# Two cross-attention layers on one core: inner matmuls padded to 128 rows and columns, softmax probabilities split two key tiles at a time

## The reference, cut to what matters

```python
# layer 0: 8 heads of 64 channels; x and context are (16, 128, 512)
q = einsum('oc,bcn->bon', Wq, x);  kv = einsum('oc,bcm->bom', Wkv, context)
sim = einsum('bhdi,bhdj->bhij', q, k)          # 512 queries x 512 keys
attn = softmax(sim, axis=-1)
out = einsum('bhij,bhdj->bhid', attn, v);  y = einsum('oc,bcn->bon', Wout, out) + bout
# layer 1: 8 heads of 16 channels, biases, rotary embedding on q and k, scale 1/sqrt(16)
```

## Time and profile before

| | |
|---|---|
| time, median of 3 runs | 3264.57 us (3253.11 to 3277.23) |
| span of the profiled execution | 3264.8 us |
| layer 0 attention | about 80 to 1065 us |
| layer 1 attention | about 1725 to 2520 us |
| busy over the whole span | TensorE 2477.9, VectorE 2300.3, ScalarE 1842.6, GpSimd 1806.1 us |
| mean granted TensorE clock | 0.881 of full speed |

### The profile page before, as it was taken

One profiled execution on the slowest core, in us unless ns is written; L12 is line 12 of the kernel. 1 busy time (PEld: TensorE's weight loads), 2 busy tenths in 40 slices (PEclk: granted clock), 3 DMA queues, 4 the chain that ended last, 5 costly groups with the idle time before them and its releaser, 6 DMA issues. The chain is left out here.

```text
span 3264.8 us, 41636 instructions
## 1 busy us (share of the span) xinstructions
PE 2477.9 (76%) x11034; PEld 962.1 (29%) x11062; DVE 2300.3 (70%) x3282; ACT 1842.6 (56%) x3160; POOL 1806.1 (55%) x1577
## 2 busy tenths in 40 slices
PE   2999999999999046676647888989888312999930
PEld 0333333333333023233221222222222311555510
DVE  4778878878877775675636999888996571666644
ACT  1888888888888012232225888888887301444410
POOL 1667767767767010110125889888887275333445
PEclk9999999999999568898876999899998556999975
DMA  4232222222220300000001111111110103777745
GB/s 111 54 61 57 48 60 58 49 60 59 49 57 18 154 14 1 0 0 0 0 24 36 36 31 31 35 31 31 35 29 7 55 1 105 245 244 241 242 143 171
DMA packets 145405, 219.01 MB, mean 67 GB/s; under 512 B 20232, under 2 KB 108808, under 8 KB 144144
## 3 DMA queue, kind: packets, MB, share of 16 engines
q1 hardware_dynamic: 130448, 175.83, 20.5%
q0 software_dynamic: 14848, 41.99, 4.7%
HBM read 125.41 MB, written 42.02 MB: 51 GB/s over the span
## 5 line engine op out<-in xcount | busy, mean ns | idle before, releaser
L354 POOL TENSOR_TENSOR a_p_l<-a_probs,a_p_h 128x512 f16<-128x512 f32 x1024 | 1190.5, 1175 | 416.7 <-ACT a_p_h L564 414.7
L631 DVE TENSOR_REDUCE a_negmax<-a_ps_max 128x1 f32<-128x512 f32 x1024 | 675.7, 682 | 106.7 <-PE a_ps_max L431 101.9
L558 ACT ACTIVATE a_probs<-a_ps_st 128x512 f32<-128x512 f32 x1024 | 593.6, 593 | 236.4 <-PE a_ps_st L43 228.5
L564 ACT ACTIVATE a_p_h<-a_probs 128x512 f16<-128x512 f32 x1024 | 635.2, 626 | 1.3
L465 PE MATMUL a_ps_o<-a_p_h,a_v_h 128*128 128x512 f16 x1024 | 402.9, 393 | 1.9 <-POOL a_p_l L354 1.9
L679 DVE RECIPROCAL a_sums<-a_sums 128x128 f32<-128x128 f32 x384 | 356.3, 938 | 20.1 <-ACT a_plain L576 20.1
L890 POOL TENSOR_TENSOR f_hl<-f_h,f_hh 128x2048 f16<-128x2048 f32 x16 | 65.1, 4071 | 375.5 <-ACT f_hh L994 375.5
L431 PE MATMUL a_ps_max<-a_k_st,a_q_st 48*128 48x512 f16 x512 | 210.9, 413 | 32.9 <-DVE a_negmax L631 16.6
L43 PE MATMUL a_ps_st<-a_q_st,a_k_st 68*128 68x512 f16 x512 | 208.7, 408 | 6.9 <-ACT a_probs L558 6.2
L467 PE MATMUL a_ps_o<-a_p_h,a_v_l 128*64 128x512 f16 x512 | 206.3, 403 | 0.0
L470 PE MATMUL a_ps_o<-a_p_l,a_v_l 128*128 128x512 f16 x512 | 205.8, 402 | 0.0
(11 more groups left out here) (293 smaller groups left out, 4717.7 us busy)
## 6 DMA issues: line engine op xcount, KB each, us to landing
s_raw<-in_guT SPq DMA_DIRECT2D x32, 768.0 KB, 5.7
m_y<-s_y SPq DMA_DIRECT2D x32, 768.0 KB, 4.8
a_k_hh<-a_qk_h SPq DMA_DIRECT2D x64, 256.0 KB, 5.1
a_ctx_in<-in_ctx SPq DMA_DIRECT2D x32, 256.0 KB, 2.6
a_q_hl<-a_qk_h SPq DMA_DIRECT2D x32, 256.0 KB, 4.4
a_q_hm<-a_qk_h SPq DMA_DIRECT2D x32, 256.0 KB, 4.7
a_q_hl<-a_qk_l SPq DMA_DIRECT2D x32, 256.0 KB, 5.0
a_k_lo<-a_qk_l SPq DMA_DIRECT2D x32, 256.0 KB, 5.0
```

The costliest lines, as they stand in the source:

```text
L354: pool.tensor_tensor(p_l[:, h % 2, j, :], probs[:, h % RAWS, j, :], p_h[:, h % 2, j, :], ALU.subtract).then_inc(p_split, 1)
L558: act.activation(probs[:, h % RAWS, j, :], ps_st[:, j % 2, :], ACT.Exp, scale=1.0 if L0 else DH1 ** -0.5).then_inc(exped, 1)
L564: act.activation(p_h[:, h % 2, j, :], probs[:, h % RAWS, j, :], ACT.Copy).then_inc(p_high, 1)
L631: dve.tensor_reduce(negmax[:, h % 2, t:t + 1], ps_max[:, t % 2, :], AX.X, ALU.max, negate=True).then_inc(maxed, 1)
```

## The change

Four things:

- Layer 0: `v_l`, 64 columns for each head before, has 128, of which 64 are filled with zeros once (a second memset on GpSimd, a second count of `cleared`), and its product with `p_h` writes all 128 rows of `a_ps_o`. VectorE writes the 64 columns inside the wider rows.
- Layer 1: the rows with the maxima move from partition 64 to 96 (`MR`), and `max_product` reads `MR` = 96 rows instead of 48, of which 48 to 95 are zeros. `score_products` reads 100 rows instead of 68.
- Both layers: `low_probs` and `high_probs` run over two key tiles at once (128 x 1024), and their counters `p_high` and `p_split` count pairs.
- ScalarE's order: the copy of tiles 0 and 1 stands behind the third exponential of the head, that of tiles 2 and 3 at the head's end, where four copies stood behind exponentials 1, 2, 3 and at the end. `normalise` stands behind the first pair on GpSimd, where it stood behind the first tile.

```diff
...
     NQK = 8 if L0 else 4
-    MR = 64
+    MR = 64 if L0 else 96
     STACKS = 12 if L0 else 6
...
         v_h = sb("v_h", [P, 2, KD, H, P], F16)
-        v_l = sb("v_l", [P, 2, KD, H, DH0 if L0 else P], F16)
+        v_l = sb("v_l", [P, 2, KD, H, P], F16)
         if not L0:
...
         SETS = 1 if L0 else 16
-        CLEARS = 1 if L0 else 4
+        CLEARS = 2 if L0 else 4
         block = ctx.enter_context(nc.Block())
...
-            def low_probs(batch, h, j):
-                need(pool, p_high, KD * (H * batch[0] + h) + j + 1)
-                pool.tensor_tensor(p_l[:, h % 2, j, :], probs[:, h % RAWS, j, :], p_h[:, h % 2, j, :], ALU.subtract).then_inc(p_split, 1)
+            def low_probs(batch, h, i):
+                need(pool, p_high, 2 * (H * batch[0] + h) + i + 1)
+                two = slice(2 * i, 2 * i + 2)
+                pool.tensor_tensor(p_l[:, h % 2, two, :], probs[:, h % RAWS, two, :], p_h[:, h % 2, two, :], ALU.subtract).then_inc(p_split, 1)
...
                 for h in range(H):
-                    for j in range(KD):
-                        low_probs(batch, h, j)
+                    for i in range(KD // 2):
+                        low_probs(batch, h, i)
                         m, p = normalised(batch, h)
-                        if j == 0 and m is not None and exists(m):
+                        if i == 0 and m is not None and exists(m):
                             normalise(m[0], p)
...
                 pool.memset(v_h[:, :, :, :, :], 1.0).then_inc(cleared, 1)
+                pool.memset(v_l[:, :, :, :, :].rearrange("p a k h n -> p a (k h) n").bitcast(F32), 0.0).then_inc(cleared, 1)
             else:
...
                 else:
-                    a, bb = q_st[0:3 * DH, par, h, c], k_st[0:3 * DH, par, h, :]
+                    a, bb = q_st[0:MR, par, h, c], k_st[0:MR, par, h, :]
                 nc.tensor.matmul(ps_max[:, t % 2, :], a, bb, start=True, stop=True).then_inc(max_scores, 1)
...
                         need(pe, v_out, n + 1)
-                need(pe, p_split, KD * g + j + 1)
+                need(pe, p_split, 2 * g + j // 2 + 1)
                 first, last_head = (L0 or h % 2 == 0) and j == 0, (L0 or h % 2 == 1) and j == KD - 1
...
                 if L0:
-                    nc.tensor.matmul(ps_o[0:DH0, u % 2, :], v_l[:, par, j, h, :], ph, start=False, stop=False)
+                    nc.tensor.matmul(o, v_l[:, par, j, h, :], ph, start=False, stop=False)
                     ins = nc.tensor.matmul(o, vh, pl, start=False, stop=last_head)
...
-                need(act, p_split, KD * (g - RAWS) + j + 1)
+                need(act, p_split, 2 * (g - RAWS) + j // 2 + 1)
                 need(act, scores, 4 * g + j + 1)
...
-            def high_probs(batch, h, j):
+            def high_probs(batch, h, i):
                 g = H * batch[0] + h
-                need(act, weighted, KD * (g - 2) + j + 1)
-                need(act, exped, 4 * g + j + 1)
-                act.activation(p_h[:, h % 2, j, :], probs[:, h % RAWS, j, :], ACT.Copy).then_inc(p_high, 1)
+                two = slice(2 * i, 2 * i + 2)
+                need(act, weighted, KD * (g - 2) + 2 * i + 2)
+                need(act, exped, 4 * g + 2 * i + 2)
+                act.activation(p_h[:, h % 2, two, :], probs[:, h % RAWS, two, :], ACT.Copy).then_inc(p_high, 1)
...
                         exponential(batch, h, j)
-                        if j > 0:
-                            high_probs(batch, h, j - 1)
+                        if j == 2:
+                            high_probs(batch, h, 0)
                         if j == 3:
...
                                 value_highs(nxt[0], nxt[1])
-                    high_probs(batch, h, KD - 1)
+                    high_probs(batch, h, 1)
                     if h == SPLIT and exists(n2):
...
                         vals = lambda a: a.rearrange("p (h d) -> p h d", h=H)
-                        dve.scalar_tensor_tensor(v_l[:, par, t - 8, :, :], vals(ps_misc[:, :]), 1 / WS, v_h[:, par, t - 8, :, 0:DH0],
+                        dve.scalar_tensor_tensor(v_l[:, par, t - 8, :, 0:DH0], vals(ps_misc[:, :]), 1 / WS, v_h[:, par, t - 8, :, 0:DH0],
                                                  ALU.mult, ALU.subtract).then_inc(lows, 1)
```

## The result

The changed kernel takes 3499.89 us (median of 4 runs, 3498.97 to 3504.75) against 3263.12 us (4 runs, 3253.11 to 3277.23): ratio 1.072, 95% interval 1.069 to 1.075. It is 7.2% slower; 3468 us was forecast, with a range of 3310 to 3590. The profiled span is 3497.3 us, 232.5 more than before's 3264.8.

The account below looks back on a forecast made before the run. Layer 0 was taken as bound by TensorE, layer 1 by nearly every engine in turn. Chain 117, layer 0 clock 32, layer 1 net 3, waits 30 and layer 1 clock 21 sum to +203 us: 3468 us, range 3310 to 3590.

Parts of the forecast that it names:

- layer 0 was forecast at +149: Layer 0's attention: 117 us from later pair results plus 32 us from TensorE's clock falling.
- layer 1 at +54: Layer 1's attention: 3 us net, 30 us of VectorE waits for GpSimd and 21 us of clock falls.
- The chain in layer 0: Layer 0: take-outs, projection and next exponentials wait behind pair copy, subtraction and normalisation; +7.8 us a batch, +117 us.
- the signs: Listed trace marks of being right: starts 0.22 us apart, layer 0 TensorE under 85% busy, heads_out waits, heads' lengths.
- Layer 0's clock: TensorE standing longer in layer 0 drops its clock, between 0 and 1 fall a batch; 32 us, range 0 to 64.
- The waits: Waits for heads_out: take-out 2.5 to 3.5 us, three times a batch; projection 3 to 5 (layer 0), 2 to 3 (layer 1).
- the forecast's 0.2 + 2: Layer 1, a batch: net +0.2 us from later projection against shorter TensorE slots, +2 us of VectorE waits for GpSimd.
- The clock's 21 us: Layer 1: clock falls rise from 4 to 9 in 15 batches, 4.3 us each; 21 us, at most 47.
- The 30 us of waits for GpSimd: Layer 1: four VectorE instructions a batch wait for longer GpSimd instructions; 2 us a batch, 30 us in all.
- Rival 1: Pair results arrive in time, so the padding's gain shows in both layers: 3163 us; chance 0.11.
- Rival 2: ScalarE's idle time absorbs half the layer 0 delay, only heads 3 and 7 lose: 3250 to 3300 us; chance 0.10.
- Rival 3: TensorE at 1.2 GHz for most of layer 0, heads 4 and 5 doubling from 6.6 to 13: 3570 us; chance 0.10.

Follow-up runs that it names:

- the run that keeps TensorE busy: Changed kernel plus unused products in layer 0 where TensorE stands, 14 in head 7 and 16 ahead of the output projection: 3448.2 us.
- padding alone: Kernel before with only the wider v_l and the 96 maxima rows, copies and subtractions one key tile at a time: 3249.9 us.
- the run with a gap: Kernel before with the padding only, plus a GpSimd wait in layer 1's head 0, ahead of the fourth subtraction, for VectorE's rotation addition: 3177.4 us.

## Why the prediction was right

Direction, place and mechanism hold. The sum (+203) is 30 us under the span's difference, but that it comes so near is partly luck: layer 0 was forecast at +149 and cost 203, layer 1 at +54 and cost 23, and the two misses cancel for the greater part. The stretch between the layers, 7 us longer, is in no term.

**The chain in layer 0, head by head.** The third exponential of each head after the change, ScalarE in order of time (the first is head 6's at 503.36, shown above):

```profile
513.13 0.60 ACT L560 ACTIVATE a_probs<-a_ps_st 128x512 f32<-128x512 f32 x1 [0.65 <-PE a_ps_st L43]
521.63 0.59 ACT L560 ACTIVATE a_probs<-a_ps_st 128x512 f32<-128x512 f32 x1
531.56 0.60 ACT L560 ACTIVATE a_probs<-a_ps_st 128x512 f32<-128x512 f32 x1 [0.88 <-POOL a_p_l L355]
538.68 0.60 ACT L560 ACTIVATE a_probs<-a_ps_st 128x512 f32<-128x512 f32 x1 [0.85 <-POOL a_p_l L355]
548.61 0.60 ACT L560 ACTIVATE a_probs<-a_ps_st 128x512 f32<-128x512 f32 x1 [0.87 <-POOL a_p_l L355]
563.77 0.59 ACT L560 ACTIVATE a_probs<-a_ps_st 128x512 f32<-128x512 f32 x1
570.75 0.60 ACT L560 ACTIVATE a_probs<-a_ps_st 128x512 f32<-128x512 f32 x1 [0.28 <-POOL a_p_l L355]
578.48 0.59 ACT L560 ACTIVATE a_probs<-a_ps_st 128x512 f32<-128x512 f32 x1
```

| step | predicted us | measured us |
|---|---|---|
| head 6 to 7 | 9.4 | 9.77 |
| 7 to 0 | 6.45 | 8.50 |
| 0 to 1 | 10.0 | 9.93 |
| 1 to 2 | 6.9 | 7.12 |
| 2 to 3 | 10.0 | 9.93 |
| 3 to 4 (with the projection) | 8.45 + 4.4 | 15.16 |
| 4 to 5, 5 to 6 | 6.8, 6.65 | 6.98, 7.73 |
| sum | 69.1 | 75.1 |

Of the 6.0 us of difference the two steps 7 to 0 and 3 to 4 have 4.4, and they are the two with a half-clock stretch: the projection is 2.66 us longer (6.09 against 3.43), and in head 7 twelve products start 0.43 apart instead of 0.22, 2.5 us, of which 2.05 show. So without the clock a batch would take some 70.4 us: **the chain is worth +9.1 a batch, not +7.8**. This is a working, not a measurement, but the run that keeps TensorE busy bears it out: there the step 7 to 0 takes 6.65 us and 6 to 7 takes 9.45, next to the prediction's 6.45 and 9.4. The chain's largest miss is head 5 to 6, 1.1 us. Heads 4 and 5 do take 6.60 us each on TensorE, but head 6's third exponential comes 5.56 us behind its transpose (at 572.92), where 4.4 was taken: ScalarE's pair copy of head 5 stands ahead of head 6's exponentials until 575.5, and an evacuation that waits for TensorE stands ahead of the third one:

```profile
577.98 0.60 ACT L531 ACTIVATE a_v_h<-a_ps_misc 128x512 f16<-128x512 f32 x1 [0.92 <-PE a_ps_misc L43]
```

Of the signs, TensorE's busy share in layer 0 is 81%, under the 85 named, and from transpose to transpose heads 2 and 3 are longer and 4 and 5 shorter, as said; head 0 isn't longer (6.92 us for 7.50), its delay shows in head 1 (8.94).

**Layer 0's clock** was mis-sized: 2.1 us a batch taken, about 4.7 by the working above, 70 us in all in place of 32. The prediction allowed for one fall a batch at most, and two came, so its range for the term (0 to 64) ended short. The run that keeps TensorE busy gives back 3.6 of the 4.7; the 0.9 us that its added products hold up the projection are most of the rest. Chain 137 and clock 70, less 3 in the first batch, make 204 us; 202.6 were measured.

**The waits** came as forecast: take-out 3.1 us, measured 2.97, three times a batch; projection about 4, measured 4.02; layer 1's projection 2 to 3, measured 3.06 to 3.3, a little more, against 0.80 before.

**Layer 1**: 54 us forecast, 23.3 measured. A batch without a fall went from 47.6 to 49.5, near the forecast's 0.2 + 2: head 4 with the projection is 1.5 us longer, heads 1 and 2 together 1.6, the others 1.3 shorter. The clock's 21 us aren't there, and this is the term that was too large: the mean granted clock of layer 1 is 0.94 against 0.93. Falls come in about every second batch, but those of before were as costly in all (98 us at half clock against 116). The layer's first batch, 8 us shorter than before, is in no term. The 30 us of waits for GpSimd can't be seen in VectorE's sum (668.45 us busy against 666.52); they moved. The rotation's addition, in head 1, went from a median of 694 ns to 1159, and L670 (now L673), which is hidden behind the projection, from 1161 to 422. That the longer additions make heads 1 and 2 longer is likely, but no run separates it:

```profile
L660 DVE TENSOR_TENSOR a_rot_a<-a_rot_a,a_rot_b x32: 691/1159/2331, 1911.1 to 2666.2; 128x512 f32<-128x512 f32 x32
```

**Rivals.** Rival 1 (the padding's gain comes through) is what happens with the normalisation first: 3184 us against its 3163. The prediction took the padding's worth in layer 0 at 4.9 us a batch when nothing else is in the way; padding alone gave 3.7 (59.5 us over 16 batches). Rival 2, half of the chain absorbed, is refuted by the table above: the steps out of heads 6, 0 and 2 take 9.8 to 9.9 us, where they took 6.7 to 7.5. Rival 3 had the right mechanism, with two falls a batch, but heads 4 and 5 stayed at full clock.

## What to carry to other kernels

Making two operations into one wide one saves its overhead and delays whatever stands behind it in the queue. Before pairing, look for the short instruction behind it that somebody waits for, and put that ahead: here the changed kernel was 7.2% slower than before with the normalisation behind the pair and 2.6% faster with it ahead. And a gain in one engine's slots must be tried by layer: padding gave 60 us in one layer and took 49 in the other, by moving a VectorE instruction under a run of GpSimd's; one wait more on GpSimd turned those 49 us of loss into 26 of gain.

## What the runs showed of the hardware

A VectorE instruction with two SBUF operands can wait for a whole unbroken run of GpSimd instructions: 5.27 us for five of them, where 0.69 is its own time. The Trainium skill ("GPSIMD Engine Reference", Key points) says that the two engines share SBUF interfaces and contend for such instructions; the trace agrees, and the run with a gap gives the price. It isn't a rule for every such run. In the kernel before the same addition begins inside a row of six subtractions without a gap and gets in behind the one under way:

```profile
2139.65 7.17 POOL L354 TENSOR_TENSOR a_p_l<-a_probs,a_p_h 128x512 f16<-128x512 f32 x6
...
2141.61 0.85 DVE L657 TENSOR_TENSOR a_rot_a<-a_rot_a,a_rot_b 128x512 f32<-128x512 f32 x1
```

There GpSimd gives way instead: the next of the six subtractions takes 1.60 us in place of 1.15. What decides which of the two gives way isn't settled by these runs; both additions began 0.8 to 0.9 us after the start of the subtraction under way.
